# Layer 1's x1 turned to rows by VectorE's 32x32-block transposes in place of TensorE's transposes and ScalarE's copies

## The chip, the cores and the metric

The kernel runs on 1 core of one Trainium2 chip. The metric is the device time of one launch in microseconds (us). Of the kernel before there are three runs; the median of them stands for its time.

## What is computed

128 graphs of 128 nodes with 512 features go through two layers of attention over each graph's adjacency matrix. The second layer is the one that the change touches:

```python
# layer 0: 8 heads, scores + soul_bias + log(adjacency + eps), softmax, x1 = attention output + x
# layer 1, node_fts = x1:
q = node_fts @ Wq + bq
k = node_fts @ Wk + bk
scores = jnp.einsum('bod,bid->boi', q, k) / denom
mask = rel_edges == 0
scores = jnp.where(mask, -1e+18, scores)
attn = jax.nn.softmax(scores, axis=2)
attn = jnp.where(mask, 0.0, attn)
ctx = jnp.einsum('boi,bie->boe', attn, node_fts) @ Wc
x = node_fts + ctx
out = (x - mu) * jax.lax.rsqrt(var + 1e-05) * gamma + beta
```

Everything is float32. To keep the precision, the large products run as three products of rounded parts (hi x hi, lo x hi, hi x lo, lines 204 to 206).

## The kernel before

The 128 graphs are taken four at a time: 32 groups, of which group t is in layer 0 while group u = t - 1 is in layer 1. Such a pair of halves is a *step*. Steps t = 0 and 1 are written out, 28 steps run as 14 turns of a loop of two steps each, and two more steps and a last one with layer 1 alone follow. So 31 steps hold a layer 0 beside a layer 1 (t = 1 to 31), and the last has layer 1 alone (`layer1_alone`). Each engine has its own list of instructions in an order written out by hand; semaphores with fixed counts (`nth(name, t, k)`) tie the lists together. No scheduler moves anything.

Layer 0 leaves x1 transposed, in `x1T`: feature on the partition, chunk c of 128 features and column (graph, node) behind it. Layer 1 needs x1 in rows too, in `x1n` (node on the partition, one row of 512 features for each graph): for the row term of the scores (`row_terms`, line 1011, VectorE: the product of each row with `v1_b`, summed into `r_c`), and for the residual and the layer norm (line 1060 and after). It gets the rows this way: `xw(g)` on TensorE turns four 128x128 tiles of `x1T` into one bank of PSUM (line 559; in the last step line 428), and `x1_out(g)` on ScalarE copies the bank to `x1n` (line 755). There is one such bank in the steady steps, so `xw(g)` waits for `x1_out(g - 1)`.

The order around it, in a steady step:

- TensorE: K and Q of chunk 1 for layer 0, `gw(0)`, `xw(0)`, `gw(1)`, `xw(1)`, the turning of the probabilities (line 398), `sa(0)`, `gw(2)`, `xw(2)`, `sa(1)`, `gw(3)`, `xw(3)`, `sa(2)`, the scores of chunk 1, `sa(3)`, `yw(0)`, `yw(1)`, `project_k(t, 2)`, and then the transposes of layer 1's attention matrix `att1` (line 621), which wait for VectorE's `dve_att1`. After them come `project_q(t, 2)`, a turning, and the products `cx` with the attention.
- VectorE: the low parts of K and Q of chunk 1 (lines 918, 926), the gates of two graphs of the next step (lines 985, 988), the four `row_terms` (line 1011), the maxima of chunk 1 (line 952), the masked scores of layer 1 (lines 1019 to 1034), the reciprocals, `attention1` (lines 1038, 1041: it ends `att1`), the low parts of y (line 1054) and of K, and `att1T_low` (line 1048).
- ScalarE: `g_out` and `x1_out` in turn, the exponentials of chunk 1, and those of layer 1 once VectorE has its maxima.

`x1n` also holds the finished rows of the step before until they have been stored to DRAM (SyncE, line 298, semaphores `s_out`). `x1_out(g)` waits for the store of its own graph.

Of the kernel before, what the change touches and what calls it, by code (L numbers as in the profile page):

```python
# [25 lines left out]
P = 128  # L26
# [4 lines left out]
C = D // P  # L31
GG = 4
NG = GRAPHS // GG
COLS = GG * P
PAIR = 2 * GG
HALF = PAIR // 2
EPS_ADJ = 1e-9
EPS_LN = 1e-5
# [11 lines left out]
def gnn_program(nc, xT, x, adj, wq, wk, wv, wqT1, wkT1, wc, bq0, bk0, bv0, wg, bg, bq1, bk1,  # L50
# [5 lines left out]
    ACT = mybir.ActivationFunctionType  # L56
# [4 lines left out]
    with ExitStack() as ctx:  # L61
# [6 lines left out]
        def flat(t):  # L68
# [17 lines left out]
        x1T = sb("x1T", [P, C, COLS])  # L86
# [5 lines left out]
        x1n = sb("x1n", [P, GG, D])  # L92
# [19 lines left out]
        ident = sb("ident", [P, P])  # L112
# [19 lines left out]
        bank = [ctx.enter_context(nc.psum_tensor(f"bank{i}", [P, 512], f32)) for i in range(8)]  # L132


        PER = dict(pe_q=4, pe_k=4, pe_cb=1, pe_s=8, pe_t=8, pe_v=4, pe_pv=4, pe_g=4, pe_x=4, pe_sa=1,
                   pe_y=4, pe_tp=1, pe_ctx=4,
                   act_q=4, act_k=4, act_exp=2 * C, act_pt=2 * C, act_x1=4, act_g=4, act_x1n=4,
                   act_y=4, act_ln=1, act_exp1=1, act_tp=1, act_nrm=4,
                   dve_q=4, dve_k=4, dve_b=1, dve_max=2 * C, dve_rcp=2 * C, dve_v=4, dve_pv=4,
                   dve_x1=4, dve_a=4, dve_r=4, dve_mask=1, dve_sa=1, dve_sub=1, dve_max1=1,  # L140
                   dve_rcp1=1, dve_att1=1, dve_tp=1, dve_y=4, dve_res=4, dve_bn=4, dve_mean=4,
                   dve_x=4, act_x=4, pool_p=2 * C, pool_eps=4, pool_rstd=4, pool_nmr=4,
                   pool_gam=4, pool_out=4)
        s = {n: sem(n) for n in PER}
        s_xT = [sem(f"xT_loaded{i}") for i in range(2)]
# [2 lines left out]
        s_out = [sem(f"out_stored{i}") for i in range(GG)]  # L148
# [19 lines left out]
        def nth(name, t, k=0):  # L168

            return t * PER[name] + k + 1  # L170


        def g_bank(c, last):
            return bank[(2, 3, 0, 1)[c] if last else 2 + c % 2]

        def x_bank(g, last):
            return bank[(7, 5)[g % 2] if last else 1]

        def sa_bank(last):
            return bank[6 if last else 0]  # L180
# [136 lines left out]
        def _(pe):  # L317
# [97 lines left out]
            def layer1_alone(u):  # L415
# [7 lines left out]
                def y_part(g, d):  # L423
                    return part(y_bank(g, True), act_rows(x1_hi, x1_lo, g), w_rows("c"), d)

                def xw(g):
                    for d in range(C):
                        mm = nc.tensor.transpose(x_bank(g, True)[:, d * P:(d + 1) * P],
                                                 x1T[:, d, g * P:(g + 1) * P], ident[:, :])
                    mm.then_inc(s["pe_x"], 1)  # L430

                def sa(c):
                    pe.wait_ge(s["act_g"], nth("act_g", u, c))
                    for g in range(GG):
                        cols_g = slice(g * P, (g + 1) * P)
                        mm = nc.tensor.matmul(sa_bank(True)[:, cols_g], g_sb[c % 2][:, cols_g],
                                              x1T[:, c, cols_g], start=(c == 0 and g == 0),
                                              stop=(c == C - 1), skip_group_check=True)
                    if c == C - 1:
                        mm.then_inc(s["pe_sa"], 1)  # L440


                pe.wait_ge(s["dve_x1"], nth("dve_x1", u, 1))
# [20 lines left out]
                for c in range(C):  # L464
                    g_part(c, C - 1).then_inc(s["pe_g"], 1)
                pe.wait_ge(s["act_pt"], nth("act_pt", u, 7))
                xw(0)
                xw(1)
                sa(0)
                pe.wait_ge(s["act_x1n"], nth("act_x1n", u, 0))  # L470
                xw(2)
                sa(1)
                pe.wait_ge(s["act_x1n"], nth("act_x1n", u, 1))
                xw(3)
                sa(2)
                sa(3)

# [1 line left out]
                for y in range(1, GG):  # L479
                    pe.wait_ge(s["act_g"], nth("act_g", u, y - 1))  # L480
                    if y == GG - 1:
# [3 lines left out]
                        for g in range(GG):  # L485
                            mm = nc.tensor.transpose(tp_bank(True)[:, g * P:(g + 1) * P], att1[:, g, :],
                                                     ident[:, :])
# [2 lines left out]
                        mm = y_part(y, d)  # L490
                    mm.then_inc(s["pe_y"], 1)
                pe.wait_ge(s["dve_tp"], nth("dve_tp", u))
                pe.wait_ge(s["act_x1n"], nth("act_x1n", u, 3))
                for g in range(GG):
                    pe.wait_ge(s["dve_y"], nth("dve_y", u, g))
                    hi_lo(ctx_bank(g, True)[:, :], [(att1T_hi[:, g, :], att1T_lo[:, g, :])],
# [2 lines left out]
            def body(it):  # L499
# [49 lines left out]
                        pe.wait_ge(s["act_g"], nth("act_g", u, c - 2))  # L549
                    hi_lo(g_bank(c, False)[:, :], w_cols("m", c), act_cols(x1_hi, x1_lo)).then_inc(s["pe_g"], 1)  # L550

                def xw(g):

                    if g == 0:
                        pe.wait_ge(s["dve_k"], nth("dve_k", t, 1))
                    else:
                        pe.wait_ge(s["act_x1n"], nth("act_x1n", u, g - 1))
                    for d in range(C):
                        mm = nc.tensor.transpose(bank[1][:, d * P:(d + 1) * P],  # L559
                                                 x1T[:, d, g * P:(g + 1) * P], ident[:, :])  # L560
                    mm.then_inc(s["pe_x"], 1)

                def sa(c):

                    if c == 0:
                        pe.wait_ge(s["dve_q"], nth("dve_q", t, 1))
                    pe.wait_ge(s["act_g"], nth("act_g", u, c))
                    for g in range(GG):
                        cols_g = slice(g * P, (g + 1) * P)

                        mm = nc.tensor.matmul(bank[0][:, cols_g], g_sb[c % 2][:, cols_g], x1T[:, c, cols_g],  # L571
                                              start=(c == 0 and g == 0), stop=(c == C - 1),
                                              skip_group_check=True)
                    if c == C - 1:
                        mm.then_inc(s["pe_sa"], 1)

                def yw(g):

# [9 lines left out]

                if not first:
                    gw(0)  # L590
                    xw(0)
                    gw(1)
                    xw(1)
                    pe.wait_ge(s["dve_pv"], nth("dve_pv", u, 3))
                    pe.wait_ge(s["act_pt"], nth("act_pt", u, 7))
                else:
                    pe.wait_ge(s_lo["m"], 2)
                turn(t, 0)
                if not first:
                    sa(0)  # L600
                    gw(2)
                    xw(2)
                    sa(1)
                    gw(3)
                    xw(3)
                    sa(2)
                scores(t, 1)
                if not first:
                    sa(3)

                    yw(0)
                    yw(1)
                    pe.wait_ge(s["act_x1n"], nth("act_x1n", u, 3))
                project_k(t, 2)
                if not first:
                    pe.wait_ge(s["dve_sa"], nth("dve_sa", u))
# [52 lines left out]
        def _(act):  # L669
# [69 lines left out]
            def body(it):  # L739
                t, u, last = it.t, it.u, not it.l0  # L740

                def g_out(c):
                    if it.second and c == 0:
                        act.wait_ge(s_cst1, 2)
                    act.wait_ge(s["pe_g"], nth("pe_g", u, c))
                    if last and c >= 2:
                        act.wait_ge(s["pe_x"], nth("pe_x", u, c))
                    nc.scalar.activation(g_sb[c % 2][:, :], g_bank(c, last)[:, :], ACT.Identity,  # L748
                                         bias=u1_c[:, c:c + 1]).then_inc(s["act_g"], 1)

                def x1_out(g):
                    act.wait_ge(s["pe_x"], nth("pe_x", u, g))
                    if not it.second:
                        act.wait_ge(s_out[g], 16 * u)
                    nc.scalar.activation(x1n[:, g, :], x_bank(g, last)[:, :], ACT.Copy).then_inc(s["act_x1n"], 1)  # L755

                def y_out(g):
                    act.wait_ge(s["pe_y"], nth("pe_y", u, g))
# [23 lines left out]
                    q_high(t, 1)  # L782
                if it.l1:
                    g_out(0)
                    x1_out(0)
                    g_out(1)
                    x1_out(1)
                if it.l0:
                    turned(t, 0)
                if it.l1:  # L790
                    if last:
                        x1_out(2)
                        g_out(2)
                        x1_out(3)
                        g_out(3)
                    else:
                        g_out(2)
                        x1_out(2)
                        g_out(3)
                        x1_out(3)  # L800
                if it.l0:
                    exps(t, 1)
                if it.l1:
# [64 lines left out]
        def _(dve):  # L868
# [130 lines left out]
            def body(it):  # L999
                t, u, last = it.t, it.u, not it.l0  # L1000

                def row_terms(g):

                    dve.wait_ge(s["act_x1n"], nth("act_x1n", u, g))
                    if g > 0:
                        dve.wait_ge(s["dve_r"], nth("dve_r", u, g - 1))
                    elif it.nxt:
                        dve.wait_ge(s["dve_a"], nth("dve_a", t + 1, 1))
                    else:
                        dve.wait_ge(s["dve_a"], nth("dve_a", NG - 1, 3))  # L1010
                    nc.vector.tensor_tensor_reduce(out=scratch[:, :], in0=x1n[:, g, :], in1=v1_b[:, :],  # L1011
                                                   scale=1.0, scalar=r0_c, op0=ALU.mult, op1=ALU.add,
                                                   accum_out=r_c[:, g:g + 1]).then_inc(s["dve_r"], 1)

                def masked_scores():
# [4 lines left out]
                    nc.vector.tensor_scalar(scratch[:, :], flat(adj_sb[par_u]), 0.0, MASKED, ALU.is_equal,  # L1020
                                            ALU.mult).then_inc(s["dve_mask"], 1)
                    dve.wait_ge(s["dve_mask"], nth("dve_mask", u))
                    dve.wait_ge(s["pe_sa"], nth("pe_sa", u))
                    for g in range(GG):
                        op = nc.vector.scalar_tensor_tensor(out=att1[:, g, :],
                                                            in0=sa_bank(last)[:, g * P:(g + 1) * P],
# [63 lines left out]
                if it.nxt:  # L1090
                    dve.wait_ge(s["dve_a"], nth("dve_a", t, 3))
                    gates(t + 1, (0, 1))
                if it.l1:
                    for g in range(GG):
                        row_terms(g)
                if it.l0:
# [195 lines left out]
```

## Time and profile before

| | |
|---|---|
| median of 3 runs | 2609.55 us |
| the three runs | 2608.56, 2609.55, 2609.57 us |
| span of the profiled execution | 2612.4 us |
| mean granted TensorE clock in it | 0.987 |
| busy: TensorE, its weight loads | 97%, 82% |
| busy: VectorE, ScalarE, GpSimd | 63%, 55%, 28% |
| DMA | 119.71 MB, mean 46 GB/s |

The profiled execution has no time of its own beside its span, from its first to its last instruction; the span lies 2.85 us above the median. The busy shares are averages over the launch, and the steady steps are alike to a few hundredths of a microsecond, so that a time within one step can be read for all of them. The trace names a wait after the instruction that ended it; "issue" is time in which an engine waited for nothing that the trace shows.

### The profile page before, as it was taken

The page shows a single profiled execution, that of the slowest core. Times are in us where ns is not written, and L with a number is a line of the kernel's source. Part 1 is how long each engine was busy: PE and PEld are TensorE (multiplying, and loading weights), DVE is VectorE, ACT ScalarE, POOL GpSimd, SP SyncE. Part 2 cuts the span into 40 slices and gives each one's busy share as a digit, 9 for nine tenths or more (in the row PEclk, how much of TensorE's full clock was granted, in tenths as well). Part 3 has the DMA queues.
Part 4 walks back from the last instruction along what each step waited for, and adds up shares of the span by engine and source line. Part 5 has one row for each costly group of instructions (what it writes and reads, how often), then busy time and mean ns, then how long its engine had stood idle before and what let it go on. Part 6 is the DMA issues. An engine that isn't in the chain of part 4 may idle for free.

```text
span 2612.4 us, 43457 instructions
## 1 busy us (share of the span) xinstructions
PE 2544.3 (97%) x14544; PEld 2132.4 (82%) x14544; DVE 1643.2 (63%) x5472; ACT 1442.4 (55%) x3858; POOL 743.5 (28%) x1024
## 2 busy tenths in 40 slices
PE   7999999999999999999999999999999999999997
PEld 5888888788887888888888887888878888888886
DVE  5566656666566665657666566665666656666655
ACT  4465545565455655556555555555555555565554
POOL 0132223332223322233323233222333223332223
PEclk9999999999999999999999999999999999999999
DMA  5010111110111101111011111011110111110100
GB/s 186 29 53 21 53 46 43 51 47 27 49 49 42 53 25 49 45 42 53 26 49 46 53 41 52 23 53 46 41 54 25 49 46 52 42 53 21 53 9 33
DMA packets 63198, 119.71 MB, mean 46 GB/s; under 512 B 6272, under 2 KB 22784, under 8 KB 58752
## 3 DMA queue, kind: packets, MB, share of 16 engines
q1 hardware_dynamic: 62976, 116.75, 12.7%
q8 instruction: 139, 2.28, 0.4%
q14 instruction: 83, 0.68, 0.1%
HBM read 83.17 MB, written 33.55 MB: 45 GB/s over the span
## 4 chain that ended last, share of the span: by engine, by line
PE 96%; issue 2%; DVE 1%; SPq 1%; DMA 0%; ACT 0%
PE bank L204 27%; PE bank L205 26%; PE bank L206 26%; PE bank L410 5%; PE bank L571 4%; PE bank L398 4%; PE bank L559 2%; PE bank L522 1%; PE bank L621 1%; DMA gamma_b<-in_gamma 0%; PE bank L324 0%; PE bank L346 0%; SPq L270 0%; PE bank L334 0%; DVE x1n L1060 0%
## 5 line engine op out<-in xcount | busy, mean ns | idle before, releaser
L1193 POOL TENSOR_TENSOR probs<-probs,rcp 128x512 f32<-128x512 f32 x256 | 275.4, 1097 | 1177.3 <-DVE rcp L962 1177.3
L722 ACT ACTIVATE probs<-probs,nmax 128x128 f32<-128x128 f32 x1024 | 396.9, 389 | 134.7 <-DVE nmax L952 134.7
L918 DVE SCALAR_TENSOR_TENSOR k_lo<-bank,cols,k_hi 64x512 fp32r<-64x512 f32 x256 | 191.8, 749 | 196.5 <-ACT k_hi L707 194.7
L1011 DVE CUSTOM_DVE_ANT_0 scratch<-x1n,v_b,consts 128x512 f32<-128x512 f32 x128 | 96.2, 752 | 309.5 <-ACT x1n L755 308.1
L707 ACT ACTIVATE k_hi<-bank,cols 64x512 fp32r<-64x512 f32 x256 | 174.8, 683 | 171.3 <-PE bank L206 168.5
L204 PE MATMUL bank<-x_hi,wk_hi 128*128 128x512 f32 x512 | 216.1, 422 | 45.8 <-issue 37.7
L748 ACT ACTIVATE g_sb<-bank,consts 128x512 f32<-128x512 f32 x128 | 87.9, 687 | 305.3 <-PE bank L206 305.3
L952 DVE CUSTOM_DVE_ANT_0 probs<-bank,bias 128x128 f32<-128x128 f32 x1024 | 227.0, 286 | 4.7 <-issue 1.5
L204 PE MATMUL bank<-x_hi,wm_hi 128*128 128x512 f32 x512 | 208.8, 408 | 1.7 <-DVE x1n L1060 1.7
L205 PE MATMUL bank<-x_lo,wk_hi 128*128 128x512 f32 x512 | 209.7, 410 | 0.0
L206 PE MATMUL bank<-x_hi,wk_lo 128*128 128x512 f32 x512 | 208.0, 406 | 0.0
L204 PE MATMUL bank<-wv_hi,x_hi 128*128 128x512 f32 x512 | 205.3, 401 | 1.7 <-DVE wv_lo L901 1.7
L204 PE MATMUL bank<-wc_hi,x_hi 128*128 128x512 f32 x512 | 202.9, 396 | 0.0
L204 PE MATMUL bank<-x_hi,wq_hi 128*128 128x512 f32 x512 | 202.8, 396 | 0.0
L206 PE MATMUL bank<-x_hi,wm_lo 128*128 128x512 f32 x512 | 200.9, 392 | 0.0
L205 PE MATMUL bank<-wv_lo,x_hi 128*128 128x512 f32 x512 | 200.3, 391 | 0.0
L206 PE MATMUL bank<-wv_hi,x_lo 128*128 128x512 f32 x512 | 200.1, 391 | 0.0
L205 PE MATMUL bank<-x_lo,wq_hi 128*128 128x512 f32 x512 | 199.9, 390 | 0.0
L206 PE MATMUL bank<-wc_hi,x_lo 128*128 128x512 f32 x512 | 199.8, 390 | 0.0
L206 PE MATMUL bank<-x_hi,wq_lo 128*128 128x512 f32 x512 | 199.8, 390 | 0.0
L205 PE MATMUL bank<-x_lo,wm_hi 128*128 128x512 f32 x512 | 199.7, 390 | 0.0
L205 PE MATMUL bank<-wc_lo,x_hi 128*128 128x512 f32 x512 | 199.3, 389 | 0.0
(145 smaller groups left out, 6294.1 us busy)
## 6 DMA issues: line engine op xcount, KB each, us to landing
out<-x1n SPq DMA_DIRECT2D x128, 256.0 KB, 2.0
xn<-in_x SPq DMA_DIRECT2D x126, 256.0 KB, 4.8
xT_land<-in_xT SPq DMA_DIRECT2D x31, 1024.0 KB, 5.2
adj_sb<-in_adj SPq DMA_DIRECT2D x32, 256.0 KB, 2.8
v_sb<-in_wk SPq DMA_DIRECT2D x4, 256.0 KB, 5.9
xT_land<-in_xT SPq DMA_DIRECT2D x4, 256.0 KB, 6.1
xT_land<-in_wq SPq DMA_DIRECT2D x4, 256.0 KB, 7.1
probsT<-in_wv SPq DMA_DIRECT2D x4, 256.0 KB, 6.1
```

The lines of the kernel that those rows point to most:

```text
L204: nc.tensor.matmul(out_ap, st[0], mv[0], start=start, stop=False)
L205: nc.tensor.matmul(out_ap, st[0], mv[1], start=False, stop=False)
L206: return nc.tensor.matmul(out_ap, st[1], mv[0], start=False, stop=stop)
L398: mm = nc.tensor.transpose(bank[6 + h][:, k * P:(k + 1) * P], probs[:, h * HALF + k, :], ident[:, :])
L410: mm = nc.tensor.matmul(bank[b][e * HD:(e + 1) * HD, g * P:(g + 1) * P], v_sb[:, g, c * P + e * HD:c * P + (e + 1) * HD], probsT[c % 2][:, ...
L571: mm = nc.tensor.matmul(bank[0][:, cols_g], g_sb[c % 2][:, cols_g], x1T[:, c, cols_g], start=(c == 0 and g == 0), stop=(c == C - 1), skip_ ...
L707: op = nc.scalar.activation(k_hi[r, :, e * P:(e + 1) * P], bank[1][r, :].rearrange("p (g j) -> p g j", g=GG), ACT.Identity, bias=bk0_c[r, ...
L722: op = nc.scalar.activation(probs[:, k, :], probs[:, k, :], ACT.Exp, bias=nmax[:, k:k + 1], scale=-1.0, accum_out=sums[:, k:k + 1])
L918: op = nc.vector.scalar_tensor_tensor(out=k_lo[r, :, e * P:(e + 1) * P], in0=bank[1][r, :].rearrange("p (g j) -> p g j", g=GG), scalar=bk0 ...
L952: op = nc.vector.tensor_tensor_reduce(out=probs[:, k, :], in0=bank[4 + h][:, (k % HALF) * P:(k % HALF + 1) * P], in1=bias0[:, k // 2, :], ...
L1011: nc.vector.tensor_tensor_reduce(out=scratch[:, :], in0=x1n[:, g, :], in1=v1_b[:, :], scale=1.0, scalar=r0_c, op0=ALU.mult, op1=ALU.add, a ...
L1193: nc.gpsimd.tensor_tensor(probs[:, half, :], probs[:, half, :], rcp[:, half].unsqueeze(2).to_broadcast([P, HALF, P]), ALU.mult)\
```

## The change

`xw` and `x1_out` go, in the steady steps and in the last one. VectorE gets `x1_rows`, between the gates and `row_terms`: sixteen transposes per step, SBUF to SBUF. Such an instruction turns 32x32 blocks; each of the sixteen takes one group of 32 partitions (a) of `x1T` with the columns of one group of 32 nodes (b) out of all 16 tiles, 512 elements per partition, and writes them to the 32 partitions (b) of `x1n`. The inner loop runs over b. `x1_rows` waits for the stores of all four graphs of the step before, and `row_terms` waits for all sixteen.

```diff
+                def x1_rows():
+
+                    dve.wait_ge(s["dve_pv"], nth("dve_pv", u, C - 1))
+                    if not it.second:
+                        for g in range(GG):
+                            dve.wait_ge(s_out[g], 16 * u)
+                    for a in range(P // BLK):
+                        for b in range(P // BLK):
+                            op = nc.vector.transpose(
+                                x1n[b * BLK:(b + 1) * BLK, :, :]
+                                .rearrange("p g (c a s) -> p a c g s", c=C, a=P // BLK)[:, a, :, :, :],
+                                x1T[a * BLK:(a + 1) * BLK, :, :]
+                                .rearrange("p c (g b r) -> p b c g r", g=GG, b=P // BLK)[:, b, :, :, :])
+                    op.then_inc(s["dve_rows"], 1)
...
                 def row_terms(g):
 
-                    dve.wait_ge(s["act_x1n"], nth("act_x1n", u, g))
+                    dve.wait_ge(s["dve_rows"], nth("dve_rows", u))
...
                 if it.l1:
+                    x1_rows()
                     for g in range(GG):
                         row_terms(g)
...
                 if not first:
                     gw(0)
-                    xw(0)
                     gw(1)
-                    xw(1)
...
                     sa(0)
                     gw(2)
-                    xw(2)
                     sa(1)
                     gw(3)
-                    xw(3)
                     sa(2)
...
                 if it.l1:
                     g_out(0)
-                    x1_out(0)
                     g_out(1)
-                    x1_out(1)
```

VectorE's row in a step, from the low part of Q to the row terms, before. "ISA" rows with a one-column output read an accumulator.

```order
L926 SCALAR_TENSOR_TENSOR q_lo<-bank,consts,q_hi 128x512 [waits act_q]
L985 ISA scratch,a_c<-xn,wg_b,consts 128x512 [waits xn_loaded0,dve_a]
L985 ISA a_c 128x1
L988 ISA xn,c_c<-xn,wg_b 128x512
L988 ISA c_c 128x1
L985 ISA scratch,a_c<-xn,wg_b,consts 128x512 [waits dve_a,xn_loaded1]
L985 ISA a_c 128x1
L988 ISA xn,c_c<-xn,wg_b 128x512
L988 ISA c_c 128x1
L1011 ISA scratch,r_c<-x1n,v_b,consts 128x512 [waits dve_a,act_x1n]
```

The same place in the changed kernel, whose line numbers are lower (936 and 939 are the gates, 961 the new transposes, 977 the row terms, 863 the first instruction of the maxima):

```order
L939 ISA xn,c_c<-xn,wg_b 128x512
L939 ISA c_c 128x1
L961 STREAM_TRANSPOSE x1n<-x1T 32x4x4x32 [waits dve_pv]
L961 STREAM_TRANSPOSE x1n<-x1T 32x4x4x32 x15
L977 ISA scratch,r_c<-x1n,v_b,consts 128x512 [waits dve_a,dve_rows]
L977 ISA r_c 128x1
```

The sixteen transposes stand between the gates and the row terms, and everything behind them on VectorE, the maxima of chunk 1 and the masked scores among it, stands behind all sixteen.

TensorE, around the turning of the probabilities of chunk 0, before:

```order
L559 MATMUL bank<-ident,x1T 128x128 [waits act_x1n]
L559 MATMUL bank<-ident,x1T 128x128 x3
L398 MATMUL bank<-ident,probs 128x128 [waits pool_p,act_pt,dve_pv]
L398 MATMUL bank<-ident,probs 128x128 x3
L398 MATMUL bank<-ident,probs 128x128 [waits pool_p]
L398 MATMUL bank<-ident,probs 128x128 x3
L571 MATMUL bank<-x1T,g_sb 128x128 [waits act_g,dve_q]
```

In the changed kernel the two rows of line 559 are gone here and at the three other places of the step, and nothing else on TensorE changes its place.

## Rows read from the trace of the kernel before

**Rows 1.** The page: chain of work that ended last, by engine

```profile
PE 96%; issue 2%; DVE 1%; SPq 1%; DMA 0%; ACT 0%
```

**Rows 2.** Timeline of TensorE in one step: start us, us, engine, line, operation

```profile
1323.28 0.60 PE L559 MATMUL bank<-ident,x1T 128*128 128x128 f32 x4
1323.72 1.04 PE L398 MATMUL bank<-ident,probs 128*128 128x128 f32 x8
...
1344.21 0.60 PE L621 MATMUL bank<-ident,att 128*128 128x128 f32 x4
...
1348.19 0.48 PE L204 MATMUL bank<-y_hi,att1T_hi 128*128 128x512 f32 x1
```

**Rows 3.** Groups by line (busy us, mean ns, idle before), and the waits

```profile
L559 PE MATMUL bank<-ident,x1T 128*128 128x128 f32 x496 | 74.1, 272 | 0.0
```

```profile
DVE scratch L1011 <- ACT x1n L755: 308.1, 97, 4.2
```

**Rows 4.** Timeline of VectorE in the same step, columns as in rows 2

```profile
1321.65 0.08 DVE L988 DVE_READ_ACCUMULATOR2_ANT c_c<- 128x1 f32 x1
1321.77 0.75 DVE L1011 CUSTOM_DVE_ANT_0 scratch<-x1n,v_b,consts 128x512 f32<-128x512 f32 x1
...
1334.43 0.08 DVE L1011 DVE_READ_ACCUMULATOR2_ANT r_c<- 128x1 f32 x1
1334.60 0.29 DVE L952 CUSTOM_DVE_ANT_0 probs<-bank,bias 128x128 f32<-128x128 f32 x1
...
1341.60 1.20 DVE L1041 SCALAR_TENSOR_TENSOR att<-att,stats,mask 128x128 f32<-128x128 f32 x4
...
1347.37 0.69 DVE L1048 TENSOR_TENSOR att1T_lo<-bank,att1T_hi 128x512 fp32r<-128x512 f32 x1
```

**Rows 5.** VectorE instructions of 512 elements: two pairs, a group, one line

```profile
1298.69 1.50 DVE L918 SCALAR_TENSOR_TENSOR k_lo<-bank,cols,k_hi 64x512 fp32r<-64x512 f32 x2
...
1342.72 1.27 DVE L1054 TENSOR_TENSOR y_lo<-bank,y_hi 128x512 fp32r<-128x512 f32 x2
```

```profile
L1063 DVE BATCH_NORM_STATS2 bnst<-x1n 128x6 f32<-128x512 f32 x128 | 89.0, 695 | 4.4
```

```profile
L1020 DVE TENSOR_SCALAR scratch<-adj_sb x32: 416/420/422, 138.9 to 2586.3; 128x512 f32<-128x512 f32 x32
```

**Rows 6.** TensorE's gaps (in brackets) and its clock, last but two columns

```profile
1289.80 0.49 PE L204 MATMUL bank<-x_hi,wk_hi 128*128 128x512 f32 x1 [2.69 <-issue]
...
1290.59 0.58 PE L204 MATMUL bank<-x_hi,wk_hi 128*128 128x512 f32 x1
...
1293.96 0.44 PE L206 MATMUL bank<-x_hi,wk_lo 128*128 128x512 f32 x1
```

```profile
489.97 0.49 PE L204 MATMUL bank<-x_hi,wk_hi 128*128 128x512 f32 x1 [2.60 <-issue]
```

```profile
2251.60 0.49 PE L204 MATMUL bank<-x_hi,wk_hi 128*128 128x512 f32 x1 [2.74 <-issue]
```

```profile
2564.53 0.47 PE L204 MATMUL bank<-x_hi,wm_hi 128*128 128x512 f32 x1 [1.48 <-DVE x1n L1060]
```

```profile
1292.00:1293.00 1.00, 1.00 (x4) 0.81 (x3) 0.96 (x4) 0.99 (x2) 1.00 (x2) 0.50 0.00 0
```

```profile
490.00:492.00 2.00, 2.00 (x9) 1.66 (x10) 1.74 (x7) 1.98 (x10) 0.73 (x3) 1.00 0.04 8
```

```profile
PE bank L204 <- issue: 37.7, 13, 3.2
```

**Rows 7.** The last step: VectorE, TensorE, GpSimd, and a store's landing

```profile
2585.96 0.43 DVE L1019 TENSOR_SCALAR mask<-adj_sb 128x512 bf16<-128x512 f32 x1
...
2591.53 1.14 DVE L1041 SCALAR_TENSOR_TENSOR att<-att,stats,mask 128x128 f32<-128x128 f32 x4
```

```profile
2592.90 0.60 PE L486 MATMUL bank<-ident,att 128*128 128x128 f32 x4
```

```profile
2577.20 1.83 POOL L1220 TENSOR_TENSOR x1n<-x1n,beta_b 128x512 f32<-128x512 f32 x1
```

```profile
out<-x1n SPq DMA_DIRECT2D x128, 256.0 KB, 2.0
```

More of the change, by code:

```diff
@@ L35 @@
 PAIR = 2 * GG
+BLK = 32
 HALF = PAIR // 2
@@ L132, in gnn_program @@
         bank = [ctx.enter_context(nc.psum_tensor(f"bank{i}", [P, 512], f32)) for i in range(8)]
-        PER = dict(pe_q=4, pe_k=4, pe_cb=1, pe_s=8, pe_t=8, pe_v=4, pe_pv=4, pe_g=4, pe_x=4, pe_sa=1,
+        PER = dict(pe_q=4, pe_k=4, pe_cb=1, pe_s=8, pe_t=8, pe_v=4, pe_pv=4, pe_g=4, pe_sa=4,
                    pe_y=4, pe_tp=1, pe_ctx=4,
-                   act_q=4, act_k=4, act_exp=2 * C, act_pt=2 * C, act_x1=4, act_g=4, act_x1n=4,
+                   act_q=4, act_k=4, act_exp=2 * C, act_pt=2 * C, act_x1=4, act_g=4,
                    act_y=4, act_ln=1, act_exp1=1, act_tp=1, act_nrm=4,
@@ L141, in gnn_program @@
                    dve_rcp1=1, dve_att1=1, dve_tp=1, dve_y=4, dve_res=4, dve_bn=4, dve_mean=4,
-                   dve_x=4, act_x=4, pool_p=2 * C, pool_eps=4, pool_rstd=4, pool_nmr=4,
+                   dve_x=4, act_x=4, dve_rows=1, pool_p=2 * C, pool_eps=4, pool_rstd=4, pool_nmr=4,
                    pool_gam=4, pool_out=4)
@@ L174, in g_bank @@
             return bank[(2, 3, 0, 1)[c] if last else 2 + c % 2]
-        def x_bank(g, last):
-            return bank[(7, 5)[g % 2] if last else 1]
         def sa_bank(last):
@@ L424, in y_part @@
                     return part(y_bank(g, True), act_rows(x1_hi, x1_lo, g), w_rows("c"), d)
[L426 to L430, printed above, removed]
                 def sa(c):
@@ L438, in sa @@
                                               stop=(c == C - 1), skip_group_check=True)
-                    if c == C - 1:
-                        mm.then_inc(s["pe_sa"], 1)
+                    mm.then_inc(s["pe_sa"], 1)
                 pe.wait_ge(s["dve_x1"], nth("dve_x1", u, 1))
@@ L466, in layer1_alone @@
                 pe.wait_ge(s["act_pt"], nth("act_pt", u, 7))
-                xw(0)
-                xw(1)
                 sa(0)
-                pe.wait_ge(s["act_x1n"], nth("act_x1n", u, 0))
-                xw(2)
                 sa(1)
-                pe.wait_ge(s["act_x1n"], nth("act_x1n", u, 1))
-                xw(3)
                 sa(2)
@@ L492, in layer1_alone @@
                 pe.wait_ge(s["dve_tp"], nth("dve_tp", u))
-                pe.wait_ge(s["act_x1n"], nth("act_x1n", u, 3))
                 for g in range(GG):
@@ L550, in gw @@
                     hi_lo(g_bank(c, False)[:, :], w_cols("m", c), act_cols(x1_hi, x1_lo)).then_inc(s["pe_g"], 1)
[L552 to L561, printed above, removed]
                 def sa(c):
@@ L573, in sa @@
                                               skip_group_check=True)
-                    if c == C - 1:
-                        mm.then_inc(s["pe_sa"], 1)
+                    mm.then_inc(s["pe_sa"], 1)
                 def yw(g):
@@ L590, in body @@
                     gw(0)
-                    xw(0)
                     gw(1)
-                    xw(1)
                     pe.wait_ge(s["dve_pv"], nth("dve_pv", u, 3))
@@ L601, in body @@
                     gw(2)
-                    xw(2)
                     sa(1)
                     gw(3)
-                    xw(3)
                     sa(2)
@@ L612, in body @@
                     yw(1)
-                    pe.wait_ge(s["act_x1n"], nth("act_x1n", u, 3))
                 project_k(t, 2)
@@ L746, in g_out @@
                     if last and c >= 2:
-                        act.wait_ge(s["pe_x"], nth("pe_x", u, c))
+                        act.wait_ge(s["pe_sa"], nth("pe_sa", u, c - 2))
                     nc.scalar.activation(g_sb[c % 2][:, :], g_bank(c, last)[:, :], ACT.Identity,
                                          bias=u1_c[:, c:c + 1]).then_inc(s["act_g"], 1)
[L751 to L755, printed above, removed]
                 def y_out(g):
@@ L790, in body @@
                 if it.l1:
[L791 to L800, printed above, removed]
+                    g_out(2)
+                    g_out(3)
                 if it.l0:
@@ L1022, in masked_scores @@
                     dve.wait_ge(s["dve_mask"], nth("dve_mask", u))
-                    dve.wait_ge(s["pe_sa"], nth("pe_sa", u))
+                    dve.wait_ge(s["pe_sa"], nth("pe_sa", u, C - 1))
                     for g in range(GG):
```

## Prediction
> **What bounds the kernel now.** I read the chain of work that ended last first: 96% of it is TensorE [rows 1], so a steady step lasts as long as TensorE's list, and an instruction taken off that list is worth its whole place in it. Then the waits: VectorE waits 308.1 us in all for ScalarE's copies into `x1n`, 97 times [rows 3], which is 9.9 us in each of 31 steps and costs nothing by itself. Then the timeline of one step on both engines, for the question that decides this change: how far ahead of TensorE is VectorE where TensorE next waits for it? That is at the transposes of `att1` (line 621). They start at 1344.21 [rows 2], and VectorE ended `att1` at 1341.60 + 1.20 = 1342.80 [rows 4]. So the slack is 1.41 us in a step. Other steps show the same distance. Last, TensorE's gaps and its clock [rows 6].
>
> **What it removes.** TensorE: four times four transposes a step. The four of line 559 at 1323.28 are followed by the next work at 1323.72 [rows 2], so a group holds 0.44 us of the list, although a single one is listed at 272 ns [rows 3]: they overlap. 4 x 0.44 = 1.76 us a step, all of it on the path, 31 x 1.76 = 55 us. That would be the whole gain, if nothing took its place. ScalarE's four copies of some 0.6 us were off the path, and so is their removal. It also lets `row_terms` run without waiting for TensorE and ScalarE.
>
> **What it adds.** Sixteen VectorE instructions in a row, each h long from start to start. In front of them stands the gates' end, 1321.65 + 0.08 = 1321.73, and the next starts 0.04 after [rows 4]: 1321.77. Behind them come four row terms, each 0.67 to its accumulator's read, 0.08 for that and 0.04 to the next, 0.79, and 0.09 to the maxima (1334.51 to 1334.60) [rows 4]. The maxima then start at 1321.77 + 16h + 0.04 + 3.12 + 0.09 = 1325.02 + 16h. From there to the end of `att1` the chain is VectorE, ScalarE, VectorE with no other wait: 1342.80 - 1334.60 = 8.20 us [rows 4], and I take 0.15 more for TensorE to see it. TensorE itself is ready for the transposes of `att1` at 1344.21 - 1.76 = 1342.45. The new stall there is
>
> S = 1325.02 + 16h + 8.20 + 0.15 - 1342.45 = 16h - 9.08 us (none if negative),
>
> and a step changes by S - 1.76. So VectorE hides sixteen transposes up to h = 0.57, and the change breaks even at h = 0.68.
>
> **How long is h?** No transpose of VectorE is in the trace. Instructions of 512 elements give the bounds. Least: a single-source one from SBUF to SBUF, 0.42 [rows 5]. Most, of those that do one pass: the pair of `k_lo`, 1.50 for two, 0.75 each [rows 5]. Between them are the ones of 0.69 to 0.70 (line 1063) [rows 5]. What matters as much is whether they overlap. The pair of line 1054 takes 1.27 for two of 0.68, so the second started 0.59 after the first. The pair of `k_lo`, which goes from partitions 0 to 63 on to 64 to 127, takes 2 x 0.75 with no overlap. The new transposes change the partitions that they write at each instruction. I take them like `k_lo`, without overlap, and for the length half way between 0.695 and 0.755, which is `k_lo`'s 0.75 and a few ns from one to the next: h = 0.725. S = 11.60 - 9.08 = 2.52, a step is 0.76 us longer, and 31 steps 24 us.
>
> The Trainium skill, "VectorE: DVE Perf Modes", section "Two Vector instructions with no wait between them", says that a Vector instruction is held until all earlier ones have finished when its output starts in another group of 32 partitions than the last one. By that rule all sixteen are held; the two pairs of rows 5 agree with it. The same page's section "The three transpose paths" gives 311 ns for a transpose of 128 bf16 columns, its formula for a plain two-input instruction 291; an estimate from it is 0.695 + 0.02 = 0.715 for h, and the sum would be 5 us lower. Its rules for authors send a full 128x128 transpose to TensorE wherever PSUM will do as the target, which speaks against the change.
>
> **The clock.** TensorE idles 13 times for lack of instructions, at the loop's turn [rows 6]. After 11 of these gaps, which last 2.69 to 3.2 us, its granted clock falls to 0.50 (1.2 in place of 2.4 GHz) [rows 6]; after the gaps of 2.60 and 2.74 it stays at 1.00. After the gap of 1.48 it also stayed. While it is low, eight matmuls take 1293.96 - 1290.59 = 3.37 us where they otherwise take 8 x 0.227 = 1.82: a fall costs 1.6 us. A stall of 2.52 lies between the gap that never brought a fall and those that mostly did. Bounds: no fall, or one in each of 31 steps, 50 us. I take half of it, 25 us.
>
> **What else could be late.** `x1_rows` waits for all four stores of the step before. In steady steps these have landed more than ten microseconds earlier, since GpSimd ended its last rows long before. Behind the stall, ScalarE's and VectorE's work of layer 0's chunk 2 is shifted by 16h - 9.58 = 2.0 us (1325.02 + 16h against 1334.60), but TensorE is shifted too, by 0.76. The tightest place is `att1T_low`, done at 1348.06 [rows 4] for the product at 1348.19 [rows 2]. It hangs on the low part of K, which hangs on TensorE's `project_k` (over before the stall, hence 1.76 earlier) and on VectorE being free after `att1` and two parts of y: 1344.65 + 1.3 + 1.5 + 0.7 = 1348.1, against a product now due at 1348.19 + 0.76 = 1348.95. It doesn't bind. The turning behind it waits for GpSimd, whose start moves by 1.8 us and had some five to spare. SyncE's loads behind the mask move by as much and are not needed for 8 us.
>
> **The last step.** Here x1 has to wait: GpSimd ended the last rows of the step before at 2577.20 + 1.83 = 2579.03, the store needs 2.0 us [rows 7], so `x1_rows` starts at 2581.1. 11.6 and 3.25 us later, at 2596.0, comes the mask, which stood at 2585.96 [rows 7]: 10.0 later. `att1` ended at 2592.67, and TensorE took it at 2592.90 with little slack, so it gets it 9.6 us later. It will have idled for more than ten microseconds, and its next twelve matmuls at the low clock cost 2.4 more. 12 us in all.
>
> **The sum:** 2609.55 + 24 + 25 + 12 = 2670 us, +2.3%. All differences are taken within the profiled execution, whose span is 2.85 us over the median, and put on the median.
>
> **The rivals.**
> - *The transposes overlap (faster).* If the sixteen start 0.60 apart as the pair of line 1054 does, S = 0.52, below every gap that lowered the clock. A step loses 1.24 us, 31 lose 38, the last step gains 10: 2581 us. For it: the instructions are independent. Against it: `k_lo`. It decides as soon as h is under 0.655, where 31 x (1.76 - S) outweighs the last step.
> - *A two-element rate (faster).* At h = 0.42, S = 0: -55, and 6 for the last step: 2561 us. For it: line 1020 has this rate. Against it: the other forms don't, and turning is not a plain move.
> - *Two passes (much slower).* If filling and emptying the 32x32 blocks don't overlap, or 4-byte elements go at half the rate, h = 2 x 0.725 = 1.45: S = 14.1, +383 for the steps, 50 for the clock, 24 at the end: 3067 us. Nothing in the trace excludes it.
> - *The clock never falls:* 2645 us. *It falls in each step:* 2695 us. These are ends of the forecast's own case.
> - *No change:* h between 0.65 and 0.67 would make gains and losses meet.
>
> **How the numbers follow.** Forecast's case, no overlap and h of 0.70 to 0.76: 0.62; its own range goes from 2632 (h = 0.70: 11 us for the steps, 11 for the end, no falls) to 2710 (h = 0.755: 38, 12, 50). Overlap 0.13, two-element rate 0.04, no change 0.05, two passes or anything over h = 0.77: 0.16. The range takes in the first, the second and the fourth of these, 0.80 in all: 2575 to 2725. A measurement of this kernel can tell about 0.2%, 5 us, from no change. Faster: 0.13 + 0.04 = 0.17. Same: 0.05. Slower: 0.62 + 0.16 = 0.78.
>
> **What would show it.** The new transposes' mean spacing gives h at once, and the wait of line 621 for VectorE's `att1` gives S; they should meet S = 16h - 9.08. TensorE's matmul list should be 1.76 us shorter per step. The windows behind that wait show whether the clock falls. The forecast is wrong if the spacing is under 0.66 or over 0.76, or if the stall shows up at another line than 621.

## The result

| | median, us | runs | span of the profiled run, us |
|---|---|---|---|
| before | 2609.56 | 4 | 2612.4 |
| after | 2653.77 | 4 | 2652.8 |

The ratio is 1.0166 with a 95% interval of 1.0151 to 1.018: the changed kernel is 1.7% slower, 44 us by the medians and 40 us by the spans of the two profiled runs. The forecast was 2670 us, with 2575 to 2725 as its range.

The chain that ended last was 96% TensorE's before [rows 1]. After, a quarter of it is VectorE's, and the new transposes are its largest VectorE line. The page of the kernel after, its chain:

```profile
PE 64%; DVE 25%; issue 6%; ACT 3%; SPq 1%; DMA 0%; DVEq 0%; POOL 0%
PE bank L202 19%; PE bank L203 18%; PE bank L204 18%; DVE x1n L961 13%; PE bank L408 5%; PE bank L396 3%; DVE scratch L977 2%; ACT att L757 2%; DVE att L1007 1%; DVE probs L903 1%; DVE xn L939 1%; DVE att L991 1%; DVE scratch L936 1%; ACT q_hi L681 1%; DVE att L997 1%
```

What was VectorE's wait for ScalarE's copies [rows 3] is gone; TensorE waits instead. After, the waits of TensorE (us in total, times, longest), line 588 being the transposes of `att1` and 471 the same in the last step:

```profile
PE bank L588 <- DVE att L1007: 69.4, 30, 2.5
PE bank L202 <- issue: 37.2, 13, 3.2
PE bank L471 <- DVE att L1007: 12.2, 1, 12.2
```

The step that answers [rows 4], after. VectorE goes from the gates through the sixteen transposes and four row terms to the maxima without a wait, and ends `att1` at 1357.36:

```profile
1334.47 0.08 DVE L939 DVE_READ_ACCUMULATOR2_ANT c_c<- 128x1 f32 x1
1334.47 11.45 DVE L961 STREAM_TRANSPOSE x1n<-x1T 32x512 f32<-32x512 f32 x16
1346.08 0.75 DVE L977 CUSTOM_DVE_ANT_0 scratch<-x1n,v_b,consts 128x512 f32<-128x512 f32 x1 [0.17 <-DVE x1n L961]
...
1349.15 0.08 DVE L977 DVE_READ_ACCUMULATOR2_ANT r_c<- 128x1 f32 x1
...
1356.16 1.20 DVE L1007 SCALAR_TENSOR_TENSOR att<-att,stats,mask 128x128 f32<-128x128 f32 x4
```

TensorE in the same step and behind it, which answers [rows 2]:

```profile
1357.51 0.63 PE L588 MATMUL bank<-ident,att 128*128 128x128 f32 x4 [2.14 <-DVE att L1007]
1357.89 0.48 PE L202 MATMUL bank<-x_hi,wq_hi 128*128 128x512 f32 x1
...
1358.67 0.62 PE L202 MATMUL bank<-x_hi,wq_hi 128*128 128x512 f32 x1
1359.09 0.63 PE L203 MATMUL bank<-x_lo,wq_hi 128*128 128x512 f32 x1
1359.52 0.63 PE L204 MATMUL bank<-x_hi,wq_lo 128*128 128x512 f32 x1
```

Before, these transposes waited for nothing. Now TensorE stands still for 2.14 us, and here its clock falls behind the stall: the matmuls go from 0.23 to 0.43 us apart. The windows (the last but two columns: granted clock) show the fall itself, from full to half speed, which is 2.4 and 1.2 GHz:

```profile
1358.00:1359.00 1.00, 1.00 (x6) 0.87 (x5) 1.00 (x2) 0.74 (x2) 0.00 (x0) 0.83 0.00 0
1359.00:1360.00 1.00, 1.00 (x4) 0.71 (x3) 0.97 (x2) 0.00 (x0) 0.00 (x0) 0.50 0.00 0
```

**Where the 40 us of the spans are.**
- *Steps, about 17 us.* The stall reads 2.14 and 2.47 us in turn from one step to the next, against the 1.76 us taken off TensorE's list. From one `att1` to the next without a turn of the loop between them, it was 77.86 us before (1344.21 to 1422.07) and is 78.70 after where no clock falls (870.88 to 949.58): 0.84 more. The other kind of step has the loop's turn in it and is not alike to a few hundredths (80.50 to 82.63 us before), as the gap and the clock behind it vary. With the gap taken off it is 80.60 - 2.74 = 77.86 before (2223.75 to 2304.35) and 81.36 - 2.96 = 78.40 after (949.58 to 1030.94), both without a fall: 0.54 more. The mean is 0.69. From the first `att1` transposes to the last of a steady step (2391.46 us before, 2422.78 after) the kernel loses 31.3 us in all, 14 of them by the clock (next point), which leaves 17. The last steady step (t = 31) has no gates in front of the transposes and no stall, and gains its 1.8 us.
- *Clock, about 14 us.* Before, 11 falls at the loop's turn. After, 13 behind the stall and 7 at the loop's turn, 20 in all. A step with a fall behind its stall takes 80.3 us instead of 78.7, so 9 more falls are 9 x 1.6 = 14.
- *Last step, 12 us.* Its `att1` comes 10.2 later and its end 12.0 later than before, both counted from x1's last low part.
- *Start, -3 us.* The first transposes of `att1` stand at 143.56 against 146.47 before. In the trace of before TensorE was at its low clock for 6.8 us more in the first 100 us, before anything that the change touches.

-2.9 + 31.3 + 12.0 = 40.4 us, the difference of the spans. The medians' 44 us are of other runs, in which starts and falls differ a little.

### The profile page after: what moved, and what is told of

Read it like the earlier page. It is cut to its first block, busy times and chain, and to the rows that moved or that the text cites. A ratio compares the mean times of both kernels' runs of the same rounds, so it can differ in the third digit from the quotient of the medians.

```text
span 2652.8 us, 42728 instructions
## 1 busy us (share of the span) xinstructions
PE 2504.2 (94%) x14032; PEld 2088.1 (79%) x14032; DVE 1995.4 (75%) x5984; ACT 1376.6 (52%) x3730; POOL 743.7 (28%) x1024
## 4 chain that ended last, share of the span: by engine, by line
PE 64%; DVE 25%; issue 6%; ACT 3%; SPq 1%; DMA 0%; DVEq 0%; POOL 0%
PE bank L202 19%; PE bank L203 18%; PE bank L204 18%; DVE x1n L961 13%; PE bank L408 5%; PE bank L396 3%; DVE scratch L977 2%; ACT att L757 2%; DVE att L1007 1%; DVE probs L903 1%; DVE xn L939 1%; DVE att L991 1%; DVE scratch L936 1%; ACT q_hi L681 1%; DVE att L997 1%
## 5 line engine op out<-in xcount | busy, mean ns | idle before, releaser
L961 DVE STREAM_TRANSPOSE x1n<-x1T 32x512 f32<-32x512 f32 x512 | 359.8, 703 | 9.9 <-DMA out<-x1n 3.3
L883 DVE TENSOR_TENSOR v_sb<-bank,bv_b 128x512 f32<-128x512 f32 x128 | 88.1, 689 | 169.1 <-PE bank L408 103.9
L202 PE MATMUL bank<-x_hi,wq_hi 128*128 128x512 f32 x512 | 210.7, 412 | 0.0
L203 PE MATMUL bank<-x_lo,wq_hi 128*128 128x512 f32 x512 | 206.8, 404 | 0.0
L204 PE MATMUL bank<-x_hi,wq_lo 128*128 128x512 f32 x512 | 206.5, 403 | 0.0
```

The lines of the kernel that those rows point to most:

```text
L202: nc.tensor.matmul(out_ap, st[0], mv[0], start=start, stop=False)
L203: nc.tensor.matmul(out_ap, st[0], mv[1], start=False, stop=False)
L204: return nc.tensor.matmul(out_ap, st[1], mv[0], start=False, stop=stop)
L883: nc.vector.tensor_tensor(v_sb[:, g, :], bank[2 + g % 2][:, :], bv_b[:, :], ALU.add)\
L961: op = nc.vector.transpose(x1n[b * BLK:(b + 1) * BLK, :, :] .rearrange("p g (c a s) -> p a c g s", c=C, a=P // BLK)[:, a, :, :, :], x1T[a ...
```

## The experiments

The account to be tested: a step loses TensorE's 1.76 us and gets a stall, as long as what sixteen transposes of 0.717 us need beyond what VectorE had free, and the stalls lower the clock on top. Its rivals: that the price is paid for each transpose, with no free part; that the transposes could have overlapped; that the clock or the last step have no part in it.

**No transposes.** The whole of `x1_rows` but its waits is left out:

```diff
-                    for a in range(P // BLK):
-                        for b in range(P // BLK):
-                            op = nc.vector.transpose(...)
-                    op.then_inc(s["dve_rows"], 1)
+                    nc.vector.memset(carrier[0:1, 2 * C + GG - 1:2 * C + GG], 0.0).then_inc(s["dve_rows"], 1)
```

> The changed kernel with no transposes at all (x1n keeps old content, so layer 1's row term and residual are left wrong; the waits stay). Theory (a step loses TensorE's 1.76 us and gets back a stall that VectorE's 11.5 us cause): nothing is left to stall on, 31 x 1.76 = 55 us are gained, about 2555 us, the line of att1's transposes waits for nothing, TensorE's clock falls only after the 13 gaps at the loop's turn. Rival (the removal alone brings less, since something else is late next): over 2565 us with a new wait in the trace.

2551.99 us, ratio 0.9782 (0.9765 to 0.9798), 58 us under the kernel before. TensorE waits for VectorE no more in any steady step. From one `att1` to the next, without the loop's turn, it is 76.09 us (2323.47 to 2399.56) in place of 77.86: the removal is worth 1.77 us a step, as worked out for it, so the whole loss lies in what was added. The few us beyond 31 x 1.77 = 55 lie elsewhere: in its trace one fall of the clock less at the loop's turn, a last step shorter by 1.5, and an earlier start.

**Twelve and fourteen of sixteen.** The same loop, cut short:

```diff
                         for b in range(P // BLK):
+                            if 4 * a + b >= 12:     # or 14
+                                continue
                             op = nc.vector.transpose(
```

> Twelve of the sixteen transposes (a quarter of x1's features are not turned, so layer 1 is left partly wrong). Theory: 12 x 0.716 = 8.6 us fit before TensorE comes to att1's transposes (by 0.3 us), so there is no stall in a step and 55 us are gained; the last step ends some 7 to 8 us later: 2562 us. Rival (each transpose costs its share of time, no threshold): three quarters of the way from no transposes (2555) to all (2654), 2629 us.

> Fourteen of the sixteen transposes (an eighth of x1's features are not turned). Theory: past the threshold by about 0.8 us, so a step is 1.76 - 0.8 = 1.0 us shorter than before; the stall is too short to lower TensorE's clock; last step +10: 2589 us. Rival (no threshold): 2641 us.

Twelve: 2559.14 us (ratio 0.9809, 0.9792 to 0.9825). Fourteen: 2583.07 us (0.9885, 0.9861 to 0.991). So the first twelve transposes of each step cost 7 us in all; two more cost 24, and the last two 71. With twelve a step is as long as with none, 76.09 us (2395.83 - 2319.74), and only the last step is longer in the trace, by 11 us; the start and the loop's turns (nine falls in place of ten, shorter gaps) give 4 back. Twelve leave TensorE without a wait in the steady steps:

```profile
PE bank L202 <- issue: 35.0, 13, 2.9
PE bank L471 <- DVE att L1009: 8.9, 1, 8.9
```

Fourteen bring the first short ones:

```profile
PE bank L588 <- DVE att L1009: 26.2, 30, 1.0
```

There is a threshold, and it lies between twelve and fourteen; in the steady steps the price per transpose is zero below it. The rival without a free part (2629 and 2641 us) falls. With fourteen no step of the loop has a fall of the clock behind its stall of 0.7 or 1.0 us, in this trace. Nor are the falls at the loop's turn as many as before: five behind 13 gaps, in place of 11. The four runs go from 2575.06 us at a mean granted clock of 0.995 to 2588.08 at 0.990, so part of what fourteen gain over the kernel before is the clock's.

**Both.** TensorE's sixteen transposes are back at their places, with no ScalarE copies and no use of their result:

```diff
                 if not first:
                     gw(0)
+                    xw(0)
                     gw(1)
+                    xw(1)
...
                     gw(2)
+                    xw(2)
...
                     gw(3)
+                    xw(3)
```

> The changed kernel, with TensorE's sixteen transposes back at their places (their result is not used) and no ScalarE copies. Theory: TensorE has 1.76 us more to do in a step and stalls 1.76 us less, about 0.5 us, so the step's length is VectorE's as in the changed kernel; but a stall of 0.5 us no longer lowers the clock, so the falls go back from 20 to the 11 or so at the loop's turn: 9 x 1.6 = 14 us less than the changed kernel, about 2638 us. Rival (the clock has no part in the loss, TensorE's list counts in full): 2654 us, or up to 55 us more.

2646.12 us, ratio 1.0131 (1.0114 to 1.0148) against the 1.0166 (1.0151 to 1.018) of the change: 31 x 1.76 = 55 us of work more on TensorE, and the kernel is 8 us faster rather than slower. So it is VectorE that sets the step, and the stall is down to what was expected:

```profile
PE bank L600 <- DVE att L1019: 14.7, 30, 0.6
```

The clearest sign is the step itself: from one `att1` to the next, with no turn and no fall between, it is 78.70 us (869.56 to 948.26) with TensorE's transposes and 78.70 without them (870.88 to 949.58 in the kernel after).

The gain was 8 us (4 by the spans of the profiled runs) and not the 16 that I had expected. No fall comes behind the stall any more, and the falls are at the loop's turn alone, 12 of them; but six of these last 6.8 us in place of 3.4, so that the clock is low for 61 us of the steady steps, hardly less than the 68 of the change. After a gap of 3.09 us that ends at 1300.50, thirteen matmuls in a row run at the low clock in place of eight, and the clock is still low at 1305:

```profile
1305.00:1306.00 1.00, 1.00 (x4) 0.81 (x3) 0.00 (x0) 0.00 (x0) 0.84 (x4) 0.50 0.00 0
```

Why the clock comes back later there isn't settled: the gap is no longer than others. So this run doesn't tell much of the clock. That the clock has a part in the loss rests on the steps of the kernel after, 80.3 us with a fall and 78.7 without, and on the next run.

**Same 32 partitions.** Same number and size of transposes, each from one group of 32 partitions to the same group, four in a row before the next group. The blocks land at wrong nodes:

```diff
-                    for a in range(P // BLK):
-                        for b in range(P // BLK):
+                    for q in range(P // BLK):
+                        for a in range(P // BLK):
                             op = nc.vector.transpose(
-                                x1n[b * BLK:(b + 1) * BLK, :, :]
+                                x1n[q * BLK:(q + 1) * BLK, :, :]
...
-                                x1T[a * BLK:(a + 1) * BLK, :, :]
-                                .rearrange("p c (g b r) -> p b c g r", g=GG, b=P // BLK)[:, b, :, :, :])
+                                x1T[q * BLK:(q + 1) * BLK, :, :]
+                                .rearrange("p c (g b r) -> p b c g r", g=GG, b=P // BLK)[:, a, :, :, :])
```

> Sixteen transposes of the same size and number, but twelve of the fifteen transitions between them stay in the same 32 partitions, both read and written (each reads and writes group q; so most blocks land at wrong nodes, and layer 1 is wrong). Theory (an instruction that changes its partitions waits until the one before has finished): twelve starts come 0.61 us apart instead of 0.717, the sixteen take 10.2 us instead of 11.45, the stall shrinks to some 1.1 us, too short to lower the clock: 2609.6 - 31 x 0.8 + 11 = 2596 us. Rival (a transpose never overlaps with the next): 11.45 us and 2654 us.

2582.0 us, ratio 0.9907 (0.9886 to 0.9928): the same sixteen transposes, and 72 us less than in the change. One step's sixteen:

```profile
1296.65 9.97 DVE L961 STREAM_TRANSPOSE x1n<-x1T 32x512 f32<-32x512 f32 x16
```

9.97 in place of 11.45 us. The instructions' starts in the trace: within a group of partitions 0.63 us from the first to the second and 0.59 to the third and fourth, as the pair of line 1054 in [rows 5] did; an instruction takes 0.66 there (the first of a group 0.70), so these overlap. At the three changes of group it is 0.67, more than the 0.66 of the instruction in front: no overlap. In the real order (kernel after) all fifteen starts are 0.71 to 0.72 apart, at 0.70 of length. Twelve of those fifteen change only the group that is written, so that alone is enough to prevent the overlap. An order with its inner loop over a would change only the group that is read at twelve of the fifteen; whether those overlap no run here shows, since this one kept or changed both together. No order avoids both, as each of the sixteen has its own pair of groups.

The stall is 0.7 or 1.0 us, as with fourteen transposes. The time is 14 us under the 2596 that I had expected, and the clock is the reason: the expectation took the 11 falls at the loop's turn as given, and this trace has one. Behind a gap as long as those with a fall in [rows 6] the clock stays up:

```profile
1266.43 0.49 PE L202 MATMUL bank<-x_hi,wk_hi 128*128 128x512 f32 x1 [3.12 <-issue]
```

```profile
1268.00:1270.00 2.00, 2.00 (x11) 1.63 (x10) 1.82 (x5) 1.99 (x3) 1.92 (x4) 1.00 0.01 4
```

This makes the run the best measure of the clock's part in the change. From the first `att1` transposes to the last of a steady step it is 73.3 us shorter than the kernel after (2349.47 against 2422.78). About 43 are the steps' own length (78.70 and 77.21 us without turn or fall, 29 times), and 30 are 19 falls less at 1.6 us. The 72 us are thus not the overlap's alone.

**Last step as before.** Only the last step gets its TensorE transposes and ScalarE copies back. VectorE's part of the edit:

```diff
                 if it.l1:
-                    x1_rows()
+                    if not last:
+                        x1_rows()
```

> The changed kernel, but the last step (layer 1 alone) turns x1 on TensorE and copies on ScalarE as the kernel before did. Theory: the 12 us that the last step was found to lose come back and nothing else: 2642 us. Rival (the last step's loss is made of something else, as the stores behind): under 4 us.

2643.03 us, ratio 1.014 (1.0123 to 1.0157), 11 us under the change (12 expected). The runs of this kernel spread from 2636 to 2649, so the 11 carries an error of a few us. The traces are closer: from the last `att1` transposes of a steady step to the end it is 74.5 us before the change, 86.5 after it, and 74.5 here. The steady steps repeat what the kernel after did, with 11 falls behind 30 stalls and six at the loop's turn. The trace of after shows the mechanism, `x1_rows` waiting for the store of the step before:

```profile
2609.61 11.45 DVE L961 STREAM_TRANSPOSE x1n<-x1T 32x512 f32<-32x512 f32 x16 [3.31 <-DMA out<-x1n]
```

and TensorE behind it, 12.17 us idle and then at the low clock:

```profile
2631.53 1.09 PE L471 MATMUL bank<-ident,att 128*128 128x128 f32 x4 [12.17 <-DVE att L1007]
2632.27 0.78 PE L202 MATMUL bank<-wc_hi,x_hi 128*128 128x512 f32 x1
2632.84 0.63 PE L203 MATMUL bank<-wc_lo,x_hi 128*128 128x512 f32 x1
```

**Spread.** The step's sixteen transposes go where VectorE had nothing to do, and the last step is as before the change:

```diff
                     v_out(t, 2)
+                    if it.l1 and 2:
+                        x1_rows(0, 2)
                     v_out(t, 3)
                     recips(t, 0)
+                    if it.l1:
+                        x1_rows(2, 6)
                     k_low(t, 1)
...
                 if it.l1:
-                    x1_rows()
+                    if not last:
+                        x1_rows(6, 16)
```

> All sixteen transposes, correct, spread over VectorE's idle time in a step: two before v_out(t, 3), where it waited 2.0 us, four before k_low(t, 1), where it waited 3.3 us, ten at the place of the change; the last step as before the change. Theory (only what lies between the gates and att1 beyond 9.2 us costs anything): ten take 7.2 us, no stall is left, 31 x 1.76 us are gained and the last step loses nothing: 2554 us, 2.1% under the kernel before. Rival (the earlier six delay the low parts of K and Q, and with them TensorE): over 2565 us with a wait of the scores or of sa for VectorE.

2552.63 us, ratio 0.9785 (0.9772 to 0.9798): 2.15% under the kernel before, with all of x1 turned on VectorE. One step:

```profile
1354.93 1.40 DVE L994 STREAM_TRANSPOSE x1n<-x1T 32x512 f32<-32x512 f32 x2
1357.05 0.69 DVE L913 TENSOR_TENSOR v_sb<-bank,bv_b 128x512 f32<-128x512 f32 x1 [0.71 <-PE bank L208]
1357.92 2.85 DVE L994 STREAM_TRANSPOSE x1n<-x1T 32x512 f32<-32x512 f32 x4
1361.18 1.51 DVE L899 SCALAR_TENSOR_TENSOR k_lo<-bank,cols,k_hi 64x512 fp32r<-64x512 f32 x2 [0.42 <-ACT k_hi L691]
...
1366.68 7.16 DVE L994 STREAM_TRANSPOSE x1n<-x1T 32x512 f32<-32x512 f32 x10
```

Both early groups end before what VectorE waits for next (0.71 and 0.42 us are left of the waits), so they cost nothing, and ten remain in front of the row terms, fewer than the threshold. TensorE has no wait for VectorE in the steady steps, and the time is that of the kernel with no transposes at all, within the spread of the runs. TensorE is the bound again:

```profile
PE 96%; issue 2%; DVE 1%; SPq 1%; DMA 0%; ACT 0%
```

## Why the prediction was right

**TensorE's list.** 1.76 us a step was forecast. The kernel without transposes and the spread one both have a step of 76.09 us in place of 77.86: 1.77. Right.

**h.** Forecast 0.725, without overlap. Measured: a duration of 0.703 us, 0.717 from start to start. The pair of `k_lo` [rows 5] was the right row to read the overlap from, and the same-partitions kernel shows that it is the change of partitions that decides: 0.59 to 0.63 without, 0.717 with. The sentence of the Trainium skill that the forecast cited ("VectorE: DVE Perf Modes", "Two Vector instructions with no wait between them") is borne out on the chip by that pair of numbers, for transposes too; its estimate of 0.715 for h was nearer than mine. One detail was misread: the forecast took all sixteen as held, but the first writes to the group that the gates' last read wrote to as well, and it started 0.08 us before that read had ended (1334.47 against 1334.55). So fifteen are held.

**The stall.** S = 16h - 9.08 gives 2.39 us for the measured h; the traces show 2.14 and 2.47. It appeared at the line that was named. Three small things were off. The spacing was 0.008 us less than taken, sixteen times. The transposes started 0.12 us earlier than the row terms had, as just said. And in every other step the row terms are 0.90 us apart, not 0.79 or 0.80: a semaphore instruction (line 972) then stands in front of each in the trace, as it did before the change, where the waits for ScalarE hid it. In one such step of the kernel after:

```profile
1426.99 0.75 DVE L977 CUSTOM_DVE_ANT_0 scratch<-x1n,v_b,consts 128x512 f32<-128x512 f32 x1
1427.67 0.08 DVE L977 DVE_READ_ACCUMULATOR2_ANT r_c<- 128x1 f32 x1
1427.90 0.75 DVE L977 CUSTOM_DVE_ANT_0 scratch<-x1n,v_b,consts 128x512 f32<-128x512 f32 x1
```

From the first transpose to the maxima it takes 14.69 us in one kind of step (1334.47 to 1349.16) and 15.02 in the other (1414.47 to 1429.49), against 14.85 in the forecast. With the early start this gives 0.48 and 0.81 us more for a step in place of 0.76; measured are 0.54 and 0.84. So the steps' term, forecast as 24 us, came out as 17: the mean is 0.69, and the last steady step has no stall and gains 1.8 us, which I had not seen; the rest is the first step's and shorter gaps at the loop's turn.

**The clock.** Forecast: a fall behind half of the stalls, 25 us. There were 13 falls in 30 stalls. The half was the middle of two bounds and not worked out, so that it came near is luck. What the sum missed is that the falls at the loop's turn got fewer at the same time, from 11 to 7. It counted falls that come, and not those that go: the net is 9 falls and 14 us, and here the forecast was 11 us too long. The forecast also went by the length of a gap, and the runs show that this alone doesn't decide: with the same partitions 12 gaps of 2.6 to 3.1 us at the loop's turn had no fall behind them, while ten of the stalls of 2.14 us in the kernel after had one. What decides is open.

**The last step.** Forecast 12, measured 12.0, with the wait for the store at its beginning as described.

**Behind the stall** nothing else turned up, as forecast. Twelve transposes in a step fitted with no wait at all, as the forecast's threshold of 9.08 us says (12 x 0.717 = 8.6), and fourteen (10.0) did not.

All in all 61 us were forecast and 44 measured, 40 by the spans. Of the 21 between 61 and 40, 7 are the steps', 11 the clock's, and 3 the start's, which has nothing to do with the change. The rival with overlapping transposes had 2581 us, and the kernel that makes them overlap took 2582. That is partly luck: the rival kept all falls at the loop's turn, of which ten were gone in that kernel's trace (16 us), and against that it had the stall at 0.52 us where it was 0.7 or 1.0.

## What to carry to other kernels

Work that moves to an idle engine is free only up to the slack at the place where the bounding engine next waits for it. That slack can be read off two timelines (here 1.41 us, and 9.1 with the waits that the change itself removes), and a block of work longer than it may still be free in pieces, at the waits that the engine has elsewhere in the step: with the last step as it was, the same sixteen instructions cost 35 us in a row, and brought 56 us spread out. On the bounding engine a stall can cost more than its length, since its clock may fall behind it; and it can change how often the clock falls elsewhere, in either direction, so the falls have to be counted over the whole trace.

## What the runs showed of the hardware

- VectorE turns 32 partitions x 512 float32 elements in 32x32 blocks in 703 ns, about as long as a two-input addition of 512 elements (689 ns).
- Back to back, such instructions start 0.59 to 0.63 us apart when they read and write the same 32 partitions as the one before, and 0.717 us apart when they write to others. A change of the partitions read alone was not measured.
- TensorE's clock fell behind stalls of 2.14 and 2.47 us, in 13 of 30 (three of the falls within the last half microsecond of the stall), and in 11 of 30 in the kernel with its last step as before. Behind stalls of up to 1.0 us (fourteen transposes, the same partitions, both) there was none.
- The 13 gaps at the loop's turn, 2.6 to 3.3 us long in all kernels, had 11 falls behind them before, 7 after, 10 without transposes, 10 spread, 9 with twelve, 5 with fourteen, 12 with both, 1 with the same partitions and 6 with the last step as before. Some falls lasted 6.8 in place of 3.4 us, six of them in the kernel with both. Neither is explained.
